# Two-layer gated cross-attention: where the second layer's values are projected

## What is computed

```python
def attn(x, ctx, Wq, bq, Wk, bk, Wv, bv, Wo, bo):      # both layers, same ctx
    q = heads(layernorm(x) @ Wq.T + bq)                # 1024 rows
    k = heads(ctx @ Wk.T + bk)                         # 6404 rows
    v = heads(ctx @ Wv.T + bv)                         # 6404 rows
    a = softmax(q @ k.T / sqrt(8))                     # per head, 1024 x 6404
    return concat(a @ v) @ Wo.T + bo

x = x + tanh(g_xattn[0]) * attn(x, ctx, *layer0)
x = x + tanh(g_ffn[0]) * moe0(layernorm(x))            # gelu experts, two of eight
x = x + tanh(g_xattn[1]) * attn(x, ctx, *layer1)       # mask of all ones here
x = x + tanh(g_ffn[1]) * moe1(x)                       # gated silu experts, two of eight
```

## Time and profile before

| | |
|---|---|
| median of 3 runs | 2577.66 us (2577.53 to 2584.01) |
| the profiled execution | 2573.93 us |
| its span, first to last instruction | 2572.0 us |
| mean granted clock of PE | 0.972 |
| last head of layer 0, second layer's keys and values between its steps | about 1091 to 1173 us |
| first maximum of layer 1 | about 1338 to 1411 us |

### The profile page before, as it was taken

How to read it: one execution, slowest core, us unless ns; L and a number is a source line. 1 busy time by engine, 2 the same in 40 slices (tenths; PEclk the granted TensorE clock), 3 DMA queues, 4 the chain that set the end, 5 groups by cost and what they waited for, 6 DMA issues and landing times.

```text
span 2572.0 us, 51035 instructions
## 1 busy us (share of the span) xinstructions
PE 2500.4 (97%) x21117; PEld 957.5 (37%) x21117; DVE 2119.7 (82%) x2168; ACT 1929.0 (75%) x3549; POOL 84.1 (3%) x83
## 2 busy tenths in 40 slices
PE   8999999999999999998977999999999999999989
PEld 3433333333333333344433333333333333333343
DVE  6799999999999999834349999999999999999044
ACT  4388888888888888864320888888888888888931
POOL 4200000000000000001000000000000000000000
PEclk9799999999999999998985999999999999999999
DMA  4311111111110000013000000000000000000000
GB/s 172 113 39 39 38 39 39 38 38 38 38 37 31 28 28 28 8 75 107 22 25 0 20 29 29 29 29 29 29 29 29 29 28 28 28 28 12 1 1 9
DMA packets 36019, 92.49 MB, mean 36 GB/s; under 512 B 4196, under 2 KB 14728, under 8 KB 35528
## 3 DMA queue, kind: packets, MB, share of 16 engines
q1 hardware_dynamic: 34344, 88.79, 9.8%
q10 hardware_dynamic: 1440, 0.40, 0.1%
HBM read 73.31 MB, written 15.74 MB: 35 GB/s over the span
## 4 chain that ended last, share of the span: by engine, by line
PE 67%; DVE 31%; issue 1%; DMA 1%; ACT 0%; SPq 0%; POOL 0%; ACTq 0%; DVEq 0%; POOLq 0%
DVE m_part L814 29%; PE ps L1167 23%; PE ps L1113 20%; PE ps L1138 10%; PE ps L1274 4%; PE ps L1282 3%; PE ps L1069 1%; PE ps L1038 1%; PE ps L1103 1%; PE ps L1181 1%; PE ps L1294 1%; PE ps L1146 0%; DMA w_att<-in_wq 0%; PE ps L1078 0%; PE ps L1250 0%
## 5 line engine op out<-in xcount | busy, mean ns | idle before, releaser
L814 DVE TENSOR_REDUCE m_part<-ps 128x2 f32<-128x1024 f32 (+1 forms) x1664 | 1933.5, 1184 | 123.8 <-PE ps L1138 110.4
L637 ACT ACTIVATE probs<-ps 128x512 f32<-128x512 f32 (+1 forms) x3264 | 1759.8, 595 | 314.8 <-PE ps L1113 193.2
L1167 PE MATMUL ps<-probs,v_all 128*9 128x256 f32 x13056 | 1010.6, 381 | 1.5 <-ACT o_raw L617 0.5
L1113 PE MATMUL ps<-q_ring,k_ring 35*128 35x512 f32 x3264 | 872.3, 497 | 0.6 <-ACT q_ring L626 0.4
L1138 PE MATMUL ps<-k_ring,q_ring 33*128 33x512 f32 (+1 forms) x3328 | 724.0, 413 | 37.8 <-DVE m_part L814 25.0
L1113 PEld LDWEIGHTS ps<-q_ring,k_ring 35*128 35x128 f32 x3264 | 348.9, 183 | 710.6 <-ACT probs L637 612.3
L1167 PEld LDWEIGHTS ps<-probs,v_all 128*9 128x9 f32 x13056 | 194.3, 88 | 549.0 <-ACT probs L637 468.2
L1138 PEld LDWEIGHTS ps<-k_ring,q_ring 33*128 33x128 f32 x3328 | 347.3, 191 | 123.5 <-DVE m_part L814 95.6
L835 DVE RECIPROCAL r_den<-ps 128x8 f32<-128x8 f32 x32 | 6.7, 208 | 106.8 <-PE ps L1146 106.6
L624 ACT ACTIVATE q_ring<-ps 3x512 fp32r<-3x512 f32 x32 | 18.8, 588 | 74.1 <-PE ps L1103 73.4
L682 ACT ACTIVATE probs<-ps,b_col 128x512 f32<-128x512 f32 x32 | 20.3, 684 | 66.9 <-PE ps L1274 66.9
(11 more groups left out here) (144 smaller groups left out, 662.7 us busy)
## 6 DMA issues: line engine op xcount, KB each, us to landing
k_ring<-k_parts SPq DMA_DIRECT2D x372, 96.0 KB
k_ring<-k_parts SPq DMA_DIRECT2D x124, 112.2 KB
big<-in_mask_t SPq DMA_DIRECT2D x10, 640.0 KB, 11.8
k_parts<-k_ring SPq DMA_DIRECT2D x12, 512.0 KB, 3.1
k_parts<-big SPq DMA_DIRECT2D x12, 512.0 KB, 3.1
q_ring<-q_parts SPq DMA_DIRECT2D x120, 32.0 KB
big<-in_w SPq DMA_DIRECT2D x1, 2048.0 KB, 9.4
ctx_t<-in_w SPq DMA_DIRECT2D x1, 2048.0 KB, 10.6
```

Source lines behind the costliest of these rows:

```text
L637: A(probs[0:k, n % PSLOTS, HALF * half:HALF * half + HALF], ps[0:k, e_bank(unit), :], ACT.Exp, scale=SCALE).then_inc(sem(f"exp_done{l}"), 1)
L814: V.tensor_reduce(m_part[:, h % 2, :, p, c], mx(n % 2)[:, :, 0:chunk_w[c]], AX.X, ALU.max).then_inc(sem(f"mx_done{l}"), 1)
L1113: pe.matmul(bank, k_ring[row:row + ROWS_EXP, koff:koff + P], q_ring[row:row + ROWS_EXP, qoff:qoff + HALF], start=not masked, stop=True).th ...
L1167: mm = pe.matmul(ps[32 * g:32 * g + VW, 7, 0:QGW], v_all[:, t, h, :], probs[:, n % PSLOTS, QGW * g:QGW * g + QGW], start=(t == 0), stop=(t ...
```

## The change

- `values` of layer 1 leave `next_layer`. They now stand in `attention` for both layers, after the units 2, 6, 10, ... 50 of the first maximum. The banks are given by `v_bank`: 7 in layer 0, as before, and 4 and 5 in turn in layer 1.
- Layer 1's values are emptied by ACT, with the same `set_v`, right before its exponentials of that layer. DVE's copies go; `next_keys_values` becomes `next_keys`.
- The wait for the values moves with them: from before the last output of layer 0 to before the first scores of layer 1. The last output of layer 0 no longer waits for the last split of the keys.
- In head 15, `next_layer` comes one step earlier (steps 5, 9, ... 49 for 6, 10, ... 50).
- On DVE, the bias of 15 heads and the mask's total come before the second layer's keys.
- On SP, the wait for the values and the loads of the second layer's experts move behind `load_first1`, `attention_rows` and `build_mask`.

```diff
+        def v_bank(l, c):
+            return 4 + c % 2 if l else 7
 ...
             store_k(1)
+            load_first1()
+            sp.wait_ge(sem("bo_added"), 1)
+            sp.wait_ge(sem("o_biased0"), 2)
+            attention_rows(sp, 1)
+            build_mask()
             sp.wait_ge(sem("v_proj1"), NCH)
             sp.wait_ge(sem("k_proj1"), NCH)
             sp.dma_start(w1_1, ...)
             sp.dma_start(w2_1, ...)
-            load_first1()
-            sp.wait_ge(sem("bo_added"), 1)
-            sp.wait_ge(sem("o_biased0"), 2)
-            attention_rows(sp, 1)
-            build_mask()
             load_heads(1)
 ...
             project_q(1)                                  # ACT
+            for c in range(NCH):
+                set_v(1, c)
             exp_all(1)
 ...
-                    n = min(4, NFULL - 4 * c)             # DVE, in next_keys_values
-                    dve.wait_ge(sem("v_proj1"), c + 1)
-                    dve.wait_ge(sem("pv_done0"), min((H - 1) * NT + 4 * c + 4, H * NT))
-                    bank = ps[:, 2 + c % 2, :].rearrange("p (t h d) -> p t h d", t=4, h=H)
-                    V.tensor_copy(v_all[:, 4 * c:4 * c + n, :, 0:HD], bank[:, 0:n]).then_inc(sem("v_set1"), 1)
-                    if c == NCH - 1:
-                        V.tensor_copy(v_all[0:TAIL, NFULL:NT, :, 0:HD], bank[0:TAIL, n:n + 1]).then_inc(sem("v_set1"), 1)
 ...
-                if l == 0:                                # DVE, in maxima
-                    next_keys_values()
-                    total_mask()
                 dve.wait_ge(sem(f"b_row_in{l}"), ROW_IN)
                 dve.wait_ge(sem(f"mx_done{l}"), len(UNITS) - 1)
                 add_bias(0, C - HD)
+                if l == 0:
+                    total_mask()
+                    next_keys()
                 o_norm(l, len(UNITS) - 1, H - 1)
 ...
                 keys(1, c, 0)                             # PE, in next_layer
-                values(1, c, 2, 2)
 ...
-                    if l == 0 and i % 4 == 2 and i // 4 < NCH:
-                        values(0, i // 4, 7, 1)
+                    if i % 4 == 2 and i // 4 < NCH:
+                        values(l, i // 4)
                     if i == NU + 2:
+                        pe.wait_ge(sem(f"v_set{l}"), NCH + 1)
                         if l == 0:
-                            pe.wait_ge(sem("v_set0"), NCH + 1)
 ...
-                        if l == 0 and h == H - 1 and t >= 4 + LAG and (t - LAG) % 4 == 0:
-                            next_layer((t - LAG) // 4 - 1)
+                        if l == 0 and h == H - 1 and t > OUT_AT and (t - OUT_AT) % 4 == 1:
+                            next_layer((t - OUT_AT) // 4)
 ...
                 if l == 0:
                     next_layer(NCH - 1)
-                    pe.wait_ge(sem("k_split1"), NCH)
-                    pe.wait_ge(sem("v_set1"), NCH + 1)
                 m_unit(l, UNITS[-1], masked)
```

More of the change, by code:

```diff
@@ L584, in copy_over, with set_v @@
                       bias=one_rows[:, 0:1]).then_inc(sem("copied_over"), 1)
-            def set_v(c):
+            def set_v(l, c):
                 n = min(4, NFULL - 4 * c)
-                act.wait_ge(sem("v_proj0"), c + 1)
-                bank = ps[:, 7, :].rearrange("p (t h d) -> p t h d", t=4, h=H)
-                A(v_all[:, 4 * c:4 * c + n, :, 0:HD], bank[:, 0:n], ACT.Identity).then_inc(sem("v_set0"), 1)
+                act.wait_ge(sem(f"v_proj{l}"), c + 1)
+                bank = ps[:, v_bank(l, c), :].rearrange("p (t h d) -> p t h d", t=4, h=H)
+                A(v_all[:, 4 * c:4 * c + n, :, 0:HD], bank[:, 0:n], ACT.Identity).then_inc(sem(f"v_set{l}"), 1)
                 if c == NCH - 1:
                     act.wait_ge(sem("v_init"), 3)
-                    A(v_all[0:TAIL, NFULL:NT, :, 0:HD], bank[0:TAIL, n:n + 1], ACT.Identity).then_inc(sem("v_set0"), 1)
+                    A(v_all[0:TAIL, NFULL:NT, :, 0:HD], bank[0:TAIL, n:n + 1], ACT.Identity).then_inc(sem(f"v_set{l}"), 1)
             def std_of(tag, n=1):
@@ L709, in _ @@
                     copy_over(c + 2)
-                set_v(c)
+                set_v(0, c)
             act.wait_ge(sem("g_in"), 32)
@@ L781, in low_half, with next_keys @@
                                               in1=parts[:, 0, 0:w].bitcast(F32), op0=ALU.add, op1=ALU.subtract)
-            def next_keys_values():
+            def next_keys():
                 dve.wait_ge(*weight_in(1, "k"))
@@ L849, in maxima @@
                             whole_max(l, h)
-                if l == 0:
-                    next_keys_values()
-                    total_mask()
-                dve.wait_ge(sem(f"b_row_in{l}"), ROW_IN)
                 def add_bias(c0, c1):
@@ L859, in add_bias @@
                                     ).then_inc(sem(f"o_biased{l}"), 1)
+                dve.wait_ge(sem(f"b_row_in{l}"), ROW_IN)
                 dve.wait_ge(sem(f"mx_done{l}"), len(UNITS) - 1)
                 add_bias(0, C - HD)
+                if l == 0:
+                    total_mask()
+                    next_keys()
                 o_norm(l, len(UNITS) - 1, H - 1)
@@ L1060, in repeat, with values @@
                 mm.then_inc(sem("repeated"), 1)
-            def values(l, c, bank, banks):
+            def values(l, c):
+                banks = (1, 2)[l]
                 if c == 0:
@@ L1068, in values @@
                 for t in range(4 * c, min(4 * c + 4, NT)):
-                    mm = pe.matmul(ps[0:width(t), bank + c % banks, P * (t % 4):P * (t % 4) + P],
+                    mm = pe.matmul(ps[0:width(t), v_bank(l, c), P * (t % 4):P * (t % 4) + P],
                                    ctx_t[:, P * t:P * t + width(t)], w_att[:, l, 2, :], start=True, stop=True)
```

## The result

The changed kernel takes 2584.57 us (median of 20 runs), the kernel before in the same runs 2577.60: a ratio of 1.003, 95% interval 1.0015 to 1.0044. It is slower by 7.0 us, little beside the scatter of single runs (2571.77 to 2613.25 before, 2576.68 to 2620.29 after), but the interval leaves out 1; 2583.9 was forecast. Its profiled execution took 2582.08 us. Medians here are of all runs; ratios leave out runs that took over 1.5% longer than the fastest of their kernel.

What follows compares the result with a forecast made beforehand. PE was taken to bound layer 0's last head, DVE layer 1's first maximum at half PE clock. Terms -11.9 (passes), -0.8 (tail), +18.9 (added values) gave +6.2 us on 2577.66: 2583.9 us, range 2571 to 2591.

Steps and rivals of the forecast that it cites:

- The cost in the first maximum: Layer 1's first maximum: thirteen groups of values make DVE wait, 1.45 us a group, 18.9 us in all.
- the last group's gap: End of layer 1's first maximum: the last group, among short units, leaves DVE idle for 1.49 us.
- The premise: Layer 1's first maximum: PE's granted clock stays at 0.50, that is 1.2 GHz.
- The condition: Layer 1's first maximum: at full clock the same values would cost almost nothing, read from layer 0's first maximum.
- The passes of the last head: Layer 0's last head: twelve passes without values each save 0.99 us of PE, 11.9 us in all.
- The tail: End of layer 0's last head: an earlier reciprocal and turn of the output gain 0.8 us, between 0 and 2.07.
- The new wait for the store: Tail of layer 0's last head: ACT's copy of the turned output waits for the last keys' store, until about 1177.1 us.
- The sum: Whole kernel: -11.9 - 0.8 + 18.9 = +6.2 us, giving 2583.9 us, 0.24% more.
- Rival 1: Layer 1's first maximum: the clock rises, values fit PE's idle time, only the gain is left: 2565.0 us; chance 0.12.
- rival 2: Layer 0's last head: ACT takes PE's place, 0.6 us saved a pass instead of 0.99: 2588.6 us; chance 0.18.
- rival 3: Layer 1's first maximum: PE's idle 0.34 us a unit hides values, 0.65 us a group: 2573.5 us; chance 0.10.
- The clock's rule: Layer 1's first maximum: sustained activity should release the clock and remove the 18.9 us; layer 0's slices spoke against it.

Runs made afterwards that it cites:

- Experiments 3: Changed kernel with 14 idle matmuls in PE's wait for layer 1's queries, 2 after three of four units: 2578.57 us; the kernel before with the same: 2587.66 us.
- experiment 2: Changed kernel with one tile of layer 1's values after each of units 0 to 50, instead of four after each fourth unit: 2585.62 us, ratio 1.0058.
- experiment 5: Changed kernel with 34 and 2 idle matmuls around layer 1's first maximum, four small ones in each second step of its last head: 2568.65 us, ratio 0.9891.

## Why the prediction was right

- **The cost in the first maximum.** Forecast 18.9 us; measured 18.87 between profiles, 18.88 against the run without values. The pattern read from layer 0's row (2.01 us of PE, gaps of 1.36, 5.98 us for four units) came out to the hundredth, and so did the last group's gap, 1.48 for 1.49. The premise, a clock of 0.50, held.
- **The condition.** That the values would cost next to nothing at full clock was argued from a stage with other work in it. Experiments 3 and 5 show it in this stage, at full clock, with idle matmuls beside the values.
- **The passes of the last head.** Forecast 0.99 us saved in each, measured 6.39 - 5.50 = 0.89. What failed is the assumption that the weighing would start where the values did: keys alone hold PE for 1.06 us (1105.22 to 1106.28), where the values followed after 0.96. Over twelve passes that is 1.2 us. What holds the weighing back for these 0.10 us is not shown.
- **The tail.** The new wait for the store came as named, with a turn that starts 12.76 us earlier against head 14's reciprocal and a copy that starts only 11.95 earlier. Together head and tail gave 11.95 us where 12.7 were forecast: by the passes above 10.7 in the head, for 11.9, and the other 1.3 in the tail, for 0.8.
- **The sum.** +6.9 us in the two stages against +6.2, +7.0 in the medians. That 2583.9 lies within 0.7 us of 2584.57 is in part luck: the base, a median of three runs, came within 0.1 us of the median of twenty, whose runs scatter far more. Rival 1 (the clock rises by itself) did not occur; rival 2 fell with the passes of 5.50 us and ACT's wait of 1.21; rival 3 fell with DVE's gaps, and experiment 2 shows what became of it: PE's idle time can be used, but alternating with fills a tile costs 0.73 us. No load came late behind the experts': from the negated maximum to the end the execution took 0.57 us less than before.
- **The clock's rule.** The Trainium skill, "TensorE: Matmul & The Clock Gate", Part 1, says that sustained activity releases the clock; the rows of before spoke against it here. The runs agree in part only: PE was busy for 55.00 of 55 us at 0.50 in experiment 2, so that busy time alone does not tell it; with idle matmuls among the same work the clock was 1.00 in some executions and fell in others.

## What to carry to other kernels

Room on an engine is worth only what its clock leaves of it: before work is moved into the idle time of PE, read the granted clock of that stage, and price the work by a row at that clock (here 1.45 us a group instead of next to none). With two buffers, idle time can't be saved up: what stands between two fills counts against one unit's slack, and cut into pieces it may cost more per piece. Where such a move is wanted, keep PE working through the pause before the stage as well: with 34 idle matmuls there the stage began at full clock in four of five profiles of the changed kernel, with 14, in the one profile taken, at half. And look at several executions, since a clock that holds in one profile may fall in the next.

## What was not expected of the hardware

- PE's busy share does not show its clock: 55.00 of 55 us busy at 0.50 in experiment 2, 9.94 of 10 at 1.00 in experiment 5.
- The same code in layer 0's first maximum took 67 to 80 us over these profiles, by when the clock fell and rose; the kernel before and the changed one differ by 3.6 us there without any change to it. That is where the +2.46 of the first table arises, and why differences of some us between medians need a stage's own row.
- The clock can be lost in a last head too, where PE is paced by ACT: in the profile of experiment 2 it was 0.50 over the whole of layer 1's, and the stretch from the last reduction to the end took 217 us instead of 188.

```profile
2380.00:2400.00 20.00, 20.00 (x200) 7.38 (x198) 16.91 (x19) 18.08 (x34) 0.00 (x0) 1.00 0.01 2
2410.00:2480.00 70.00, 70.00 (x416) 17.30 (x412) 1.59 (x3) 44.31 (x83) 0.00 (x0) 0.50 0.00 1
```
